# Output bias on VectorE, expert tables as one product, and a shared unit moved to the head, in an attention and mixture-of-experts kernel

## The reference

```python
def attention(x):                       # per batch, 16 heads of 8
    q, k, v = (elu or identity)(x @ W @ W2 + biases)
    S = einsum('bhld,bhle->bhde', k, q)
    out = einsum('bhmd,bhde->bhme', v, S) / (einsum('bhld,bhld->bhl', q, k) + 1e-6)
    y = x + (out @ Wo + bo)
    return gamma * (y - mean(y)) * rsqrt(var(y) + 1e-3) + beta
def ffn(x):                             # 4096 tokens, 64 experts, 8 chosen for each token
    gates = top8(softmax(x @ wg.T)), normalised
    # expert e takes its tokens in order, at most 160 of them
    y[token] += gate * (x1 * silu(x2)) @ expert_w2[e].T,  x1, x2 = x @ expert_w1[e].T
    return shared swiglu(x) + y
result = x + attention(layernorm(x)) + ffn(layernorm(x))
```

## Time and profile before

| | us |
|---|---|
| median of 3 runs | 348.42 |
| lowest, highest | 347.32, 348.76 |
| the profiled execution | 351.51 |
| its span, first to last instruction | 349.7 |

### The profile page before, as it was taken

The page is one execution under the profiler, slowest core; times in us unless marked ns, Lnnn a source line. Parts: engine busy times, 40 slices in busy tenths (PEclk is TensorE's granted clock), DMA queues, the critical chain, the costliest instruction groups (busy, mean ns, idle before and its releaser), DMA issues.

```text
span 349.7 us, 8989 instructions
## 1 busy us (share of the span) xinstructions
PE 332.6 (95%) x2952; PEld 315.4 (90%) x2952; DVE 279.7 (80%) x1136; ACT 205.1 (59%) x449; POOL 243.8 (70%) x250
## 2 busy tenths in 40 slices
PE   8899788799999999999999999999999999989994
PEld 8888677799999999999999999999899999989982
DVE  3899996877878688888797889888879887837586
ACT  3789923556566595657475947465677566564220
POOL 5687662558878877878787778887787887766500
PEclk9999999999999999999999999999999999999999
DMA  7996653697897878797879787877878887852598
GB/s 234 337 380 243 168 116 101 222 321 199 196 208 182 201 179 207 164 228 186 210 162 232 164 208 164 208 172 195 213 167 215 183 194 188 216 99 25 101 386 266
DMA packets 57054, 70.29 MB, mean 201 GB/s; under 512 B 11952, under 2 KB 44976, under 8 KB 57008
## 3 DMA queue, kind: packets, MB, share of 16 engines
q1 hardware_dynamic: 39536, 55.55, 50.1%
q0 software_dynamic: 15360, 13.12, 26.3%
q10 hardware_dynamic: 2112, 1.05, 1.0%
HBM read 54.26 MB, written 15.43 MB: 199 GB/s over the span
## 4 chain that ended last, share of the span: by engine, by line
PE 80%; DVE 7%; DMA 4%; ACT 4%; issue 2%; POOL 1%; another core or an unknown queue 0%; POOLq 0%; SPq 0%; DVEq 0%; ACTq 0%
PE bank L1319 28%; PE bank L1329 12%; PE bank L1254 8%; PE bank L1263 4%; PE bank L1364 4%; PE bank L1338 4%; PE bank L1370 3%; PE bank L1404 2%; PE bank L1377 2%; DMA ew<-acc 2%; PE bank L1385 2%; PE bank L1293 2%; PE bank L1199 1%; PE bank L1345 1%; PE bank L1393 1%
## 5 line engine op out<-in xcount | busy, mean ns | idle before, releaser
L522 POOL DMA_INDIRECT acc<-ys,idx_g x64 | 104.9, 1639 | 32.3 <-issue 16.6
L1319 PE MATMUL bank<-xe,ew 128*128 128x160 f32 x768 | 116.8, 302 | 2.7 <-ACT xe L602 1.2
L1319 PEld LDWEIGHTS bank<-xe,ew 128*128 128x128 f32 x768 | 107.4, 190 | 4.2 <-ACT xe L602 1.4
L503 POOL DMA_INDIRECT gath<-xng,idx_g x80 | 79.8, 998 | 34.0 <-issue 21.6
L580 ACT ACTIVATE si<-bank 128x480 f32<-128x480 f32 (+1 forms) x96 | 52.1, 543 | 58.0 <-PE bank L1254 30.1
L1329 PE MATMUL bank<-ew,ac 128*128 128x128 f32 x384 | 53.5, 276 | 1.9 <-DVE ac L782 1.8
L1329 PEld LDWEIGHTS bank<-ew,ac 128*128 128x128 f32 x384 | 49.5, 192 | 3.3 <-DVE ac L782 2.0
L782 DVE TENSOR_TENSOR ac<-si,bank 128x480 f32<-128x480 f32 x64 | 41.1, 641 | 11.2 <-ACT si L580 7.5
L1254 PE MATMUL bank<-xT,shw 128*128 128x128 f32 x384 | 48.3, 276 | 0.0
L1254 PEld LDWEIGHTS bank<-xT,shw 128*128 128x128 f32 x384 | 45.4, 192 | 0.1
L613 ACT ACTIVATE ys<-bank,gath 128x128 f32<-128x128 f32 x64 | 23.3, 365 | 15.4 <-PE bank L1329 8.5
(11 more groups left out here) (170 smaller groups left out, 624.4 us busy)
## 6 DMA issues: line engine op xcount, KB each, us to landing
ew<-in_expert_w SPq DMA_DIRECT2D x64, 384.0 KB
ew<-in_expert_w SPq DMA_DIRECT2D x64, 192.0 KB
ew<-acc SPq DMA_DIRECT2D x8, 512.0 KB, 7.8
x_sb<-in_x SPq DMA_DIRECT2D x8, 256.0 KB, 6.5
xng<-xn SPq DMA_DIRECT2D x8, 256.0 KB, 4.4
acc<-zeros SPq DMA_DIRECT2D x4, 512.0 KB, 4.4
acc<-betas SPq DMA_DIRECT2D x4, 512.0 KB
gath<-xng,idx_g POOLq DMA_INDIRECT x80
```

What stands on the lines that cost most here:

```text
L503: pool.indirect_dma_start(out=gath[:, p, m, :], out_offset=None, in_=xng, in_offset=bass.IndirectOffsetOnAxis(ap=idx_g[:, g % 4, m:m + 1], ...
L522: pool.indirect_dma_start(out=acc[adds_to[g, m]], out_offset=bass.IndirectOffsetOnAxis(ap=idx, axis=0), in_=src, in_offset=None, compute_o ...
L1319: last = pe.matmul(h_view(n, half_ + 1, CAP)[:, c, :], ew[p][m][:, k * P:(k + 1) * P], xe[:, p, m, :], start=True, stop=True)
```

## The change

- `out_projection` has no bias products. `bias_rows`, `bo3` and `pick` are gone. VectorE adds `bo` to the rows `xn` of the batch ahead of `attention_y` (`offset(a)`, one instruction on 128x256).
- For q > 0, `table_hot` builds no `ohm`, and `table(q)` makes one product of `oh` with `cumB`, in which the counts of the group's four experts stand in blocks with zeros between them, 512 columns wide. `cumB` and `cumL` have three buffers; `counts_in(q)` fills one with five DMAs. Two are filled in the head, the others one in each group, behind the first weights of the next group. `cumB` is cleared once by a DMA from `zeros`.
- Nine shared units run in the head and seven behind the groups. Unit 8 has `shared_up` between `out_T(0)` and `out_projection(0)`, and `shared_down` in group 0 behind `up(0, 0)`.
- In group 0, VectorE takes `expert_mul(0, 1)` right behind `features(1)`, and `table_hot(2)` behind that.
- The root of the variances of batches 12 to 14 stays on ScalarE (now waiting for batch 14, not 15). Batch 15's is taken by GpSimd with `pow`, behind its last scatter, and `finish(15)` stands at shared unit 26, not 24.

```diff
-            def counts_l(k, first, end):
+            def counts_in(q):
+                if q > 3:
+                    sp.wait_ge(x_full, x_at['table', q - 3] + 1)
                 for m in range(M):
...
+                    sp.dma_start(cumB[32 * m:32 * m + 32, q % 3, m, :], cum_d[M * q + m, :, :]).then_inc(cumB_in[q % 3], 16)
+                sp.dma_start(cumL[:, q % 3, :], cum_d[M * q:M * q + M, :, :].rearrange("m n t -> (m n) t")).then_inc(cumB_in[q % 3], 16)
...
                 up_weights(g + 1, 0)
+                if g + 3 < NG:
+                    counts_in(g + 3)
                 sp.wait_ge(h1_full, up_at['e', g, 1] + 1)
                 up_weights(g + 1, 1)
...
             for m in (2, 3, M):
                 scatter(NG - 1, m)
 
+            n = slice(TB * (B - 1), TB * B)
+            pool.wait_ge(var2_ready, B)
+            pool.tensor_tensor(rstd2[:, n], var2[:, n], half[:, 0:TB], ALU.pow).then_inc(last_ready, 1)
...
-                n = slice(QUAD * TB * k, QUAD * TB * (k + 1))
-                act.wait_ge(var2_ready, QUAD * (k + 1))
+                end = min(QUAD * (k + 1), B - 1)
+                n = slice(QUAD * TB * k, TB * end)
+                act.wait_ge(var2_ready, end)
                 act.activation(rstd2[:, n], var2[:, n], ACT.Sqrt).then_inc(std2_ready, 1)
...
+            def offset(a):
+                n = slice(TB * a, TB * a + TB)
...
+                dve.tensor_tensor(xn[:, n, :], xn[:, n, :], bo_b.unsqueeze(1).to_broadcast([P, TB, D]), ALU.add).then_inc(xb_ready, 1)
...
+                    pe.wait_ge(cumB_in[q % 3], 16 * (M + 1) * (q // 3 + (q % 3 > 0)))
+                    last = pe.matmul(A[:, :], oh[:, 0:P], cumB[:, q % 3, :, :].rearrange("p m t -> p (m t)"), start=True, stop=True)
...
-                    pe.matmul(AQ[:, j * D:(j + 1) * D], pick[:, :], bo3[:, :], start=True, stop=False)
-                    last = pe.matmul(AQ[:, j * D:(j + 1) * D], oT_s[:, j * P:(j + 1) * P], wo_s, start=False, stop=True)
+                    last = pe.matmul(AQ[:, j * D:(j + 1) * D], oT_s[:, j * P:(j + 1) * P], wo_s, start=True, stop=True)
```

More of the change, by code:

```diff
@@ L486, in _ @@
             gates(4)
-            bias_rows()
             for r in range(NR):
                 pool.wait_ge(xn_out[r], 16)
-            for h in range(len(pieces)):
-                pool.wait_ge(gw_out[h], 16)
+            pool.wait_ge(gw_out, 16 * len(pieces))
             pool.wait_ge(pad_set, 16)
@@ L701, in _ @@
             out_copy(0)
+            silu(('s', 8))
             first_copy(0)
@@ L1075, in _ @@
             shared_add(6)
+            offset(0)
             table_hot(1)
+            shared_mul(8)
             attention_y(0)
@@ L1101, in _ @@
                     qk_inverse(a)
+                    offset(a)
                 expert_mul(g, 2)
@@ L1149, in _ @@
             finish(NG - 2)
-            for s in range(24, 27):
+            for s in range(25, 27):
                 shared_mul(s)
-                if s == 24:
+                if s == 26:
                     finish(NG - 1)
@@ L1271, in table @@
                     pe.wait_ge(cum0_done, 1)
-                if q == 1:
-                    for k in range(2):
-                        pe.wait_ge(cumL_in[k], 16 * M)
-                within = cum0[:, :] if q == 0 else cumL[:, q, :]
-                pe.wait_ge(hot_step, 4 * q + 4)
-                for m in range(M):
-                    last = pe.matmul(A[:, m * P:(m + 1) * P], ohm[:, m, :], within, start=True, stop=True)
+                pe.wait_ge(hot_step, 3 * q + 4)
+                if q == 0:
+                    for m in range(M):
+                        last = pe.matmul(A[:, m * P:(m + 1) * P], ohm[:, m, :], cum0[:, :], start=True, stop=True)
+                else:
+                    pe.wait_ge(cumB_in[q % 3], 16 * (M + 1) * (q // 3 + (q % 3 > 0)))
+                    last = pe.matmul(A[:, :], oh[:, 0:P], cumB[:, q % 3, :, :].rearrange("p m t -> p (m t)"), start=True, stop=True)
                 last.then_inc(a_full, 1)
```

95 lines of the change are left out of this document (47 added, 48 removed).

## The result

| | before | after |
|---|---|---|
| median of 7 runs | 347.65 us | 345.42 us |
| lowest, highest | 347.18, 348.77 | 345.07, 346.47 |
| profiled execution, its span | 351.51, 349.7 | 345.42, 343.6 |

The ratio is 0.9936, 95% interval 0.9914 to 0.9958: 2.2 us faster, where 5.8 were forecast. The time lies in the range, the size of the change is wrong by a factor of 2.6. The two profiled executions differ by 6.1 us, nearly what was forecast, and this agreement misleads, as will be seen.

What follows compares the result with a forecast made beforehand. TensorE's full stream was taken to bound groups 1 to 14, a chain from the groups' end the tail. Head 0.3, group 0 1.1, bias 3.3, normalisation 1.1, tail 0: 348.42 - 5.8 = 342.6 us, range 340.4 to 345.8.

Steps and rivals of the forecast that it cites:

- The ninth unit: Shared unit moved from the tail to head and group 0: hidden at both places, tail worth 0, at most 0.7 us.
- Profiled base: Profiled execution 3.1 us above the median, laid to profiling; the same microseconds saved were taken off the median of 348.42.
- The head's 1.19: TensorE's wait for `xe` until 57.15, behind the head's projection; read from the profile of before.
- Head: Unit's way up fills TensorE's 0.55 us wait for `oT_s`; gain 0.3 us, between 0 and 1.2.
- Group 0: TensorE's 1.76 us wait for the second expert's `ac` goes, less 0.67 for the unit: gain 1.1, between 0.3 and 1.5.
- Bias in groups 1 to 14: Bias products gone from TensorE's full stream: 0.22 us a batch, 3.3 us for the fifteen batches of groups 0 to 14.
- Last normalisation: Root waits for batch 14, so TensorE's 1.11 us wait for a silu in group 15 goes: gain 1.1 us.
- Tables: One product of 512 columns takes as long as four of 128: gain 0, at most 15 x 0.05 us.
- loads of counts: 75 small DMAs for 8 delay SyncE in group 0: taken as 0, at most a loss of 1 us in group 1.
- Tail: Behind the groups, VectorE's wait for a read-back sum until 338.31 sets the end; seven units worth 0, at most 0.7 us.
- B: Rival, 0.13: GpSimd's pow in the tail waits for its scatters to land; up to 2.8 us given back, 345.4.
- A: Rival, 0.15: group 1 waits for weights, or the third expert's product is late; head and group 0 bring nothing, 344.0.

Runs made afterwards that it cites:

- e7: The kernel after with eight shared units in front and eight behind, without the ninth unit in the head: 343.22 us, ratio to before 0.9875.
- e3: The kernel before with only the last normalisation changed (batch 15's root a power on GpSimd): 347.20 us, ratio to before 0.9991.
- e12: The version with eight units at both ends, with the last normalisation of before (no power on GpSimd): 346.51 us, ratio 0.9904, on another chip.
- e6: The kernel before with only the tables changed (one product of 512 columns, counts loaded in the loop): 347.75 us, ratio to before 1.0012.

## Why the prediction was wrong, by its steps

- **The ninth unit, the step that cost most.** "The unit has in effect been moved from a place where it was hidden to one where it is hidden" put it at nothing, on top of a gain of 0.3 in the head. Leaving it out (`e7`) gives 2.2 us more: 0.44 in the head, 0.64 in group 0, 0.98 in a wait for a scatter's landing behind a transfer of code, 0.24 in the tail. With it out the change gives 4.4 of the forecast 5.8.
- **Profiled base.** The step that failed first is "I take the same microseconds off the median". It noted that the execution was 3.1 us above the median and laid that to profiling; it was delay of that one execution. The head's 1.19 and the 1.55 of the earlier trace rows were such, and 0.75 of the 1.11 in group 15; its own remark, 1.2 us that no record explains, was the warning. Only those two terms hung on it, some 1 us of the forecast; the 1.76 and the bias were read rightly.
- **Head, +0.3 forecast.** Measured -0.54 (56.34 against 55.80). The wait that would hide the unit was not there in a usual execution.
- **Group 0, 1.1, and 0.22 of the bias.** Measured 0.48. The 1.76 went as said; what was late next was named wrongly, the third expert's product instead of `S_s` and the gathered rows. `e7` shows 1.12 for the same without the unit.
- **Bias in groups 1 to 14, 3.08.** Measured 2.37. 0.22 us for each product holds in every group but 4, 8 and 12, which ScalarE's loads of tables set. The earlier trace rows could not show it: with 0.2 us of waiting in 16.7 TensorE reads as full.
- **Last normalisation, 1.1.** 0.5 to 1.0 by the last scatter (0.49 in `e7`, 0.64 in `e3`, 1.0 by `e12`). In after it is lost again, -0.49 in all, by the 0.98 us of the wait for a landing.
- **Tables, 0, and loads of counts, 0 to 1.** Right on the first chips (`e6`); open on the slower ones.
- **Tail, 0.** Right: 22.72 against 22.46, and the power begins behind its scatter without a wait for the landing (321.88), so B did not occur. Tails of one kernel differ as much (22.72, 22.02 and 21.78 us in the three profiles of after).
- The sum of the terms as measured is 1.6 us between two profiles (345.2 to 343.6), 2.2 between the medians. The single edits without the unit add up to 2.8 by their ratios, 3.8 by their medians, and together give 4.4; with 0.6 to 0.8 us of uncertainty in each, that is no contradiction, nor was it taken apart further. By its number the nearest rival was B, 345.4, and that is chance, since its mechanism did not occur. In what it gives up, head and group 0, the nearest was A (344.0), but not in its cause: in after, TensorE has no wait for weights in group 1.

## What to carry over

Profile the unchanged kernel twice before pricing waits from it: when the profiled execution lies 1% above the median, the surplus sits somewhere in the timeline, and a wait that ends without a record behind it is the place to look. Work moved into a wait is free only up to the wait's usual length, here 0.47 of 1.34 us; leaving that one piece out doubled the gain, and `e7` (0.9875, and 0.998 on two slower chips) is the version to keep; on those two chips the same with the old tables was no slower (0.998 and 0.9945). Where a chain of DMAs that wait for each other sets the end, a code transfer beside one of them can make the next one 0.9 to 1.5 us late, and the end up to 1.2, so a difference of that size between two kernels may be the place of their code. And a run that takes work out of a stream moves its code as well.

## What was not expected of the hardware

- Between chips the unchanged kernel takes 347.6, 349.9, 350.9 and 351.5 us at a granted clock of about 1.00, and the change's ratio goes from 0.9936 over 0.9993 to 1.0083.
- TensorE's results can be taken up 0.8 to 1.5 us later than usual (1.74 for 0.53, 1.73 for 0.42), in both of these by ScalarE and VectorE at the same moment, with nothing recorded on ScalarE between. It stands in the first profile of before and in all ten on the slower chips. The cause stays open.
- One transfer of 16 KB of code, 0.9 to 1.3 us on one DMA engine, 2.2 to 2.6 us behind the start of an indirect DMA: the next one that waits for it starts 0.9 to 1.5 us late. At 1.0 to 1.4 us behind the start no wait follows.
- `pow` on GpSimd behind an indirect DMA starts at once; its rows have 0.73 to 1.34 us for 128x2 and 2.25 for 128x8.
- One fp16 product of 512 columns costs 0.21 us start to start, as four of 128 (0.22).
